# Swin block and plain attention block on one core: the plain block's order of work rewritten around two pairs of windows, with keys spread by transfers

## The reference

```python
def attention(xw, w_qkv, b_qkv, w_proj, b_proj):      # 8x8 windows, 6 heads of 16
    qkv = jnp.einsum('bhwc,cd->bhwd', xw, w_qkv) + b_qkv
    q, k, v = ...
    q = q * (1.0 / jnp.sqrt(jnp.float32(HEAD_DIM)))
    attn = jax.nn.softmax(jnp.einsum('bnhd,bmhd->bhnm', q, k), axis=-1)
    out = jnp.einsum('bhnm,bmhd->bnhd', attn, v).reshape(Bw, h, w, DIM_OUT)
    return jnp.einsum('bhwc,cd->bhwd', out, w_proj) + b_proj
# block:  x1 = x + attention(layernorm(x));  out = x1 + fc2(gelu(fc1(layernorm(x1))))
```

## Time and profile before

| | |
|---|---|
| median of three executions | 7636.98 us (7636.67 to 7640.51) |
| span of the profiled execution | 7641.6 us; no time of its own beside the span is listed |
| first block / second block | scores of the second block run from 4489.2 to 7598.5 us |
| PE busy over the span | 97% (7426.1 us) |
| DVE, ACT, POOL busy over the span | 83%, 84%, 67% |
| second block, 5500 to 6000 us: PE, DVE, ACT, POOL | 488, 398, 374, 282 us of 500 |
| granted TensorE clock there | 0.99 of full |
| 16 DMA engines there | 12% busy |

### The profile page before, as it was taken

One profiled execution on the slowest core, in us unless ns is written; L12 is line 12 of the kernel. 1 busy time (PEld: TensorE's weight loads), 2 busy tenths in 40 slices (PEclk: granted clock), 3 DMA queues, 4 the chain that ended last, 5 costly groups with the idle time before them and its releaser, 6 DMA issues. The chain is left out here.

```text
span 7641.6 us, 317406 instructions
## 1 busy us (share of the span) xinstructions
PE 7426.1 (97%) x113246; PEld 5558.8 (73%) x113246; DVE 6361.0 (83%) x13502; ACT 6423.1 (84%) x11836; POOL 5127.1 (67%) x6741
## 2 busy tenths in 40 slices
PE   7999999999999999999999969999999999999999
PEld 4777777777777777777777747777777777777776
DVE  5888888888888888888888848887887887887886
ACT  5999999999999999999999957777777777777777
POOL 3777777777777777777777745555555555555554
PEclk9999999999999999999999979999999999999999
DMA  0111111111111111111111001111111111111111
GB/s 21 29 29 31 30 30 29 30 30 29 30 29 30 30 29 30 29 30 30 29 30 30 27 20 27 27 27 27 27 27 27 27 27 27 27 27 27 27 27 25
DMA packets 342624, 214.43 MB, mean 28 GB/s; under 512 B 265624, under 2 KB 341144, under 8 KB 341144
## 3 DMA queue, kind: packets, MB, share of 16 engines
q1 hardware_dynamic: 341146, 194.49, 10.1%
HBM read 78.66 MB, written 77.07 MB: 20 GB/s over the span
## 5 line engine op out<-in xcount | busy, mean ns | idle before, releaser
L881 POOL TENSOR_TENSOR swin_score<-swin_score,swin_top 113x588 f32<-113x588 f32 x1024 | 1204.0, 1176 | 743.2 <-DVE swin_top L753 742.7
L624 ACT ACTIVATE swin_probT<-swin_ps_probs 128x339 f32<-128x339 f32 x2048 | 925.3, 452 | 197.3 <-PE swin_ps_probs L481 178.2
L1493 POOL TENSOR_TENSOR plain_k_heads<-plain_k_hat,plain_head_mask 96x128 f32<-96x128 f32 x1568 | 585.3, 404 | 647.7 <-ACT plain_k_hat L1357 647.7
L481 PE MATMUL swin_ps_probs<-swin_ident,swin_prob 113*128 113x113 f32 x6144 | 991.8, 270 | 6.7 <-ACT swin_probT L624 6.7
L481 PEld LDWEIGHTS swin_ps_probs<-swin_ident,swin_prob 113*128 113x128 f32 x6144 | 668.0, 141 | 355.2 <-issue 320.8
L748 DVE TENSOR_TENSOR swin_score<-swin_ps_scores,swin_bias_tab 113x588 f32<-113x588 f32 x1024 | 777.3, 759 | 175.7 <-PE swin_ps_scores L471 174.4
L753 DVE TENSOR_REDUCE swin_top<-swin_score 113x12 f32<-113x588 f32 x1024 | 768.8, 751 | 0.2
L630 ACT ACTIVATE swin_prob<-swin_score 113x588 f32<-113x588 f32 x1024 | 721.5, 705 | 5.8 <-POOL swin_score L881 2.9
L1334 ACT ACTIVATE plain_prob<-plain_score 128x384 f32<-128x384 f32 x784 | 409.6, 522 | 374.9 <-DVE plain_score L1402 372.7
L1318 ACT ACTIVATE plain_hid<-plain_ps_dense,plain_b_fc 128x512 f32<-128x512 f32 x588 | 405.3, 689 | 315.0 <-PE plain_ps_dense L1180 315.0
L784 DVE SCALAR_TENSOR_TENSOR swin_x<-swin_y,swin_y_rstd,swin_x_res 98x96 f32<-98x96 f32 x1024 | 602.1, 646 | 0.8 <-POOL swin_y_rstd L899 0.7
(11 more groups left out here) (187 smaller groups left out, 21172.4 us busy)
## 6 DMA issues: line engine op xcount, KB each, us to landing
swin_k_heads<-swin_k_hat SPq DMA_DIRECT2D x1024, 36.8 KB
plain_x_in<-between_blocks SPq DMA_DIRECT2D x784, 48.0 KB, 2.2
out_dram<-plain_x SPq DMA_DIRECT2D x784, 48.0 KB, 2.0
swin_x_in<-in_x SPq DMA_DIRECT2D x224, 136.5 KB
between_blocks<-swin_x SPq DMA_DIRECT2D x224, 136.5 KB
swin_x_in<-in_x SPq DMA_DIRECT2D x224, 19.5 KB
between_blocks<-swin_x SPq DMA_DIRECT2D x224, 19.5 KB
swin_x_in<-in_x SPq DMA_DIRECT2D x224, 2.6 KB
```

The costliest lines, as they stand in the source:

```text
L481: last = nc.tensor.transpose(psP[:, n * QT:(n + 1) * QT], prob[0:QT, p, 2 * hp:2 * hp + 2, :].rearrange('p h k -> p (h k)'), ident[0:QT, 0 ...
L624: nc.scalar.activation(to, psP[:, 0:3 * QT], ACT.Copy).then_inc(did['probT'], 1)
L881: nc.gpsimd.tensor_tensor(view, view, bcast(top[0:QT, p % 2, :], 2, WIN), ALU.subtract).then_inc(did['shifted'], 1)
L1493: last = nc.gpsimd.tensor_tensor(k_heads[0:DIM, (r + 1) % 2, w, :].rearrange('c (j k) -> c j k', j=J), bcast(k_hat[:, w * WIN:(w + 1) * WI ...
```

## The change

The first block and the launch stay. In the plain block:

- `score`, `top`, `prob` and `probT` get four buffers each, one for every pair of the group, in place of two.
- `scores(d, h)` makes the scores of two pairs at once (24 records), side by side in the three banks; `mix(d, h)` mixes two pairs at once and appends the sums. The four slots are gone; the body is one list of steps.
- The three chunks of the hidden layer stand behind one another; output is done for g-3, late in the body, not for g-4 early in it.
- `k_heads` is [128, 2, J, NT]: SP writes it with six transfers SBUF to SBUF in a group, 16 partitions of 2 KB each; everything else in it stays zero from set-up. `head_mask`, its load and POOL's eight products go.
- POOL does the normalisation of x1 (two operations of 384 elements) in place of DVE's four. The reciprocal on DVE is now that of pairs 0 and 1, Ln and Exp that of pairs 2 and 3.

```diff
-        k_heads = sb('k_heads', [128, 2, WINDOWS, J * WIN])
+        k_heads = sb('k_heads', [128, 2, J, NT])
-        score = sb('score', [128, 2, SC])
-        prob = sb('prob', [128, 2, heads, HALF])
-        probT = sb('probT', [128, 2, HP, QT])
+        score = sb('score', [128, PAIRS, SC])
+        prob = sb('prob', [128, PAIRS, heads, HALF])
+        probT = sb('probT', [128, PAIRS, HP, QT])
...
+                def spread(n, parity):
+                    sp.wait_ge(did['k_hat'], upto(n))
+                    sp.wait_ge(did['scored'], upto(n - 2, 1, 2))
+                    for band in range(BANDS):
+                        for j in range(J):
+                            rows = slice(32 * band + j * D, 32 * band + (j + 1) * D)
+                            sp.dma_start(k_heads[rows, parity, j, :], k_hat[rows, :]).then_inc(did['k_spread'], 16)
...
                 with sp.Fori(4, groups // 2) as m:
                     for k in range(2):
                         load(2 * m + k, k)
+                        spread(2 * m + k - 2, k)
                         store(2 * m + k - 8, k)
...
+                    def scores(d, h):
+                        if exists(g + d, groups):
+                            pe.wait_ge(did['q_hat'], upto(g + d))
+                            pe.wait_ge(did['k_spread'], spread_total(g + d))
+                            ug, uh = earlier_half(g + d, h)
+                            pe.wait_ge(did['shifted'], upto(ug, 2 * uh + 1, PAIRS))
+                            for p in (2 * h, 2 * h + 1):
+                                for half in range(2):
+                                    w = 2 * p + half
+                                    for band in range(BANDS):
+                                        part = slice(32 * band, 32 * band + 32)
+                                        last = nc.tensor.matmul(psS[half * HALF:half * HALF + WIN, band, p % 2 * BC:(p % 2 + 1) * BC], q_hat[part, parity(d), w * WIN:(w + 1) * WIN], k_heads[part, parity(d), :, w * WIN:(w + 1) * WIN], start=True, stop=True)
                             last.then_inc(did['scored'], 1)
...
+                    def mix(d, h):
+                        if exists(g + d, groups):
+                            pe.wait_ge(did['v_heads'], upto(g + d))
+                            pe.wait_ge(did['probT'], upto(g + d, 2 * h + 1, PAIRS))
+                            mg, mh = earlier_half(g + d, h)
+                            pe.wait_ge(did['mixedT'], upto(mg, mh, 2))
...
+                    scores(0, 0)
+                    mix(-1, 0)
+                    free(('v_heads', 0), ('hid', -4, 1, CHUNKS), ('x1', -3), ('k_hat', 0))
+                    keys(1, A)
+                    turn_probs(-1, 2)
+                    free(('x2', -4), ('hid', -4, 2, CHUNKS), ('q_hat', 0))
+                    queries(1, B)
+                    free(('k_hat', 1), ('v_heads', 0), ('hid', -4, 1, CHUNKS), ('x1', -3))
+                    project(-2, A)
+                    turn_probs(-1, 3)
+                    free(('q_hat', 1), ('x2', -4), ('hid', -4, 2, CHUNKS))
+                    hidden(-3, 0, B)
+                    free(('x1', -2), ('k_hat', 1), ('v_heads', 0), ('hid', -4, 1, CHUNKS))
+                    hidden(-3, 1, A)
+                    free(('hid', -3, 0, CHUNKS), ('q_hat', 1), ('x2', -4))
+                    hidden(-3, 2, B)
+                    scores(0, 1)
+                    mix(-1, 1)
+                    free(('hid', -3, 1, CHUNKS), ('x1', -2), ('k_hat', 1), ('v_heads', 0))
+                    values(1, A)
+                    turn_x(2)
+                    turn_probs(0, 0)
+                    free(('hid', -3, 2, CHUNKS), ('q_hat', 1), ('x2', -4))
+                    output(-3, B)
+                    turn_x1(-2)
+                    turn_probs(0, 1)
...
+                    copy_turned(-1, 1)
+                    high_x1(-3)
+                    exponentials(0, 0)
+                    bias_k(1, A)
+                    copy_turned(-1, 2)
+                    exponentials(0, 1)
                     act.preload_act_table_set(GELU_SET)
+                    copy_turned(-1, 3)
+                    gelu(-3, 0, B)
+                    gelu(-3, 1, A)
+                    gelu(-3, 2, B)
                     act.preload_act_table_set(EXP_SET)
+                    log_totals(-1, 1)
+                    exponentials(0, 2)
+                    invert_totals(-1, 1)
+                    spread_values(1, A)
+                    copy_x(2)
+                    high_x(2)
+                    copy_turned(0, 0)
+                    exponentials(0, 3)
...
+                    result(-4, B)
+                    shift(0, 0)
+                    low_x1(-3)
+                    shift(0, 1)
+                    bias_q(1, B)
+                    residual(-2, A)
+                    invert_totals(-1, 0)
+                    partial_x1(-2)
+                    normalise(-1, 0)
+                    moments_x1(-2)
+                    shift(0, 2)
+                    shift(0, 3)
+                    partial_x(3)
+                    normalise(-1, 1)
+                    moments_x(3)
+                    low_x(2)
...
+                    residual_x(1)
+                    power_x(2)
+                    norm_x(2)
+                    residual_x1(-2)
+                    power_x1(-2)
+                    norm_x1(-2)
```

More of the change, by code:

```diff
@@ L75 @@
     "sq_norm": "squared norms with their floor in SBUF", "log_norm": "their logarithm", "inv_norm": "1 / norm",
-    "reciprocal": "1 / sum of a group's last two pairs in the second block",
-    "k_heads": "a pair's keys spread over heads",
+    "reciprocal": "1 / sum of a group's first two pairs in the second block",
     "q_hat": "queries ready for the scores", "k_hat": "keys ready to be spread over heads",
@@ L1157, in _ @@
                     load(n, n % 2)
+                    if n >= 2:
+                        spread(n - 2, n % 2)
                 with sp.Fori(4, groups // 2) as m:
@@ L1184, in all_windows @@
                         return bass.AP(first.tensor, first.offset, [part, pair, [HALF, 2], column])
[L1186 to L1194, removed]
-                                    part = slice(32 * band, 32 * band + 32)
-                                    last = nc.tensor.matmul(psS[half * HALF:half * HALF + WIN, band, 0:BC], q_hat[part, r % 2, w * WIN:(w + 1) * WIN], k_heads[part, r % 2, w, :], start=True, stop=True)
-                            last.then_inc(did['scored'], 1)
@@ L1221, in turn_probs, with free @@
-                    def turn_probs(slot):
-                        tg, ts = before(g, slot, 1)
-                        if exists(tg, groups):
-                            pe.wait_ge(did['prob'], upto(tg, ts, PAIRS))
-                            rg, rs = before(tg, ts, 1)
-                            pe.wait_ge(did['probT'], upto(rg, rs, PAIRS))
+                    def free(*uses):
+                        for name, d, *place in uses:
+                            if exists(g + d, groups):
+                                pe.wait_ge(did[name], upto(g + d, *place))
+                                break
@@ new lines, in project, with hidden @@
+                    def project(d, bank):
+                        if exists(g + d, groups):
+                            pe.wait_ge(did['mixedT'], upto(g + d, 1, 2))
+                            for p in range(PAIRS):
+                                last = nc.tensor.matmul(psM[0:TT, bank, p * DIM:(p + 1) * DIM], mixedT[0:DIM, parity(d), p * TT:(p + 1) * TT], w_proj[0:DIM, :], start=True, stop=True)
+                            last.then_inc(did['proj_made'], 1)
+                    def hidden(d, c, bank):
+                        if exists(g + d, groups):
+                            pe.wait_ge(did['x1T_low'], upto(g + d))
+                            side = slice(c * 128, (c + 1) * 128)
+                            product(psM[:, bank, 0:NT], w_fc1_high[:, side], w_fc1_low[:, side], x1T_high[:, :], x1T_low[:, :]).then_inc(did['fc1_made'], 1)
@@ new lines, in output @@
+                    def output(d, bank):
+                        if exists(g + d, groups):
+                            pe.wait_ge(did['hid'], upto(g + d, CHUNKS - 1, CHUNKS))
+                            for p in range(PAIRS):
+                                for c in range(CHUNKS):
+                                    last = nc.tensor.matmul(psM[0:TT, bank, p * DIM:(p + 1) * DIM], hid[:, c, p * TT:(p + 1) * TT], w_fc2[:, c, :], start=c == 0, stop=c == CHUNKS - 1)
+                            last.then_inc(did['fc2_made'], 1)
@@ new lines, in spread_values @@
+                    def spread_values(d, bank):
+                        if exists(g + d, groups):
+                            act.wait_ge(did['v_made'], upto(g + d))
+                            act.wait_ge(did['mixed_made'], upto(g + d - 2, 1, 2))
+                            for odd in range(2):
```

(6 more changed lines are left out.)

515 lines of the change are left out of this document (228 added, 287 removed).

## The result

The changed kernel takes 7408.6 us (median of four, 7406.0 to 7413.4) against 7638.7 us before: a ratio of 0.970, 95% interval 0.968 to 0.971. That is 230 us less. The profiled execution took 7406.0 us, with a span of 7404.2.

A forecast was written before the change was run, and what follows sets the result against it. PE's own stream was taken as the bound: 15.75 us a group, −0.40 stalls, −0.92 shape changes, +0.5 wait on GELU 0, 14.95 us. Over 190 groups, with +5 once, this gave 7490 us, 8-in-10 range 7405 to 7600.

The forecast's parts named there:

- rival A: Hidden chunk 2 goes on at once without waiting for GELU 0: 7391 us at best, halfway 7440; chance 0.14.
- the wait on GELU 0: On PE, hidden chunk 2 must wait for ACT's first GELU to free a bank: +0.5 us in a group.
- PE's stream sets the pace: PE is busy 487.8 of 500 us in the second block, so savings must come from its own stream.
- Stalls that go, −0.40: PE's waits at the third slot's transposes (0.30 us) and the keys (0.10) vanish in each group, with a buffer per pair.
- Changes of shape, −0.92: Per group on PE, fewer products behind tiled work (−0.40), pair transposes behind mixes (−0.30), mixes before full-width work (−0.22).
- rival B: Shape changes on PE save nothing, only the stalls go: 7566 us, at worst 7661; chance 0.18.
- Scores have the same count and stay as they are: PE's scores, like projection, output, values and sums, cost the same after the change: no saving.
- The mix of the last pairs: PE's mix needs DVE's reciprocal: zero to 0.1 us late, taken as 0; decides only without the wait on GELU 0.
- Keys by transfers, zero: SP's six key transfers land at 10.1 us, wanted at 14.9 by the next scores: 4.8 us slack, zero cost.
- rival C: Key transfers served in series on SP's queue land late and delay PE's scores: 7815 us; chance 0.07.
- Rival D: ACT's unbroken row behind GELU 2 ends too late for the transposes of x1: 15.5 us a group, 7605 us; chance 0.08.
- Once, +5: The first group's keys come some 5 us later, a single cost at the second block's start.

The follow-up runs named there:

- e4: The changed kernel with the keys spread by POOL's eight products again in place of SP's transfers: 7392.3 us, ratio 0.968 to the kernel before.
- e12: The changed kernel with the key transfers behind the group's four stores on SP's queue: 7409.0 us, ratio 0.970 to the kernel before.
- e1: The kernel before with four score, top, prob and probT buffers and nothing else moved: 7644.9 us against 7641.5 us, ratio 1.0004.
- e3: The changed kernel with two score, prob and probT buffers in place of four: 8122 us, ratio 1.063 to the kernel before.
- e8: The changed kernel with the moves of e5 and e6, and the second scores split in two behind hidden chunks 0 and 1: 7479.8 us, ratio 0.980.
- e5: The changed kernel with ACT's exponentials of pair 1 behind the three GELUs and the second table load: 7382.0 us, ratio 0.966.
- e6: The changed kernel with pair 1's transposes ahead of those of x1 on PE at the body's end: 7366.4 us, ratio 0.964.
- e9: The changed kernel with the moves of e5 and e6, and pair 3's transposes between hidden chunks 1 and 2, their copy behind GELU 1: 7336.5 us.
- e2: The kernel before with the keys spread by six SP transfers in place of POOL's products, other engines' order untouched: 8544 us, ratio 1.118.
- e11: The changed kernel with ACT's two waits ahead of the biased keys in the other order: 7403.1 us, ratio 0.969 to the kernel before.

## Why the prediction was right, and where it was off

Forecast 7490 us in a range of 7405 to 7600; measured 7408.6, 3.6 us inside the fast edge of the range and near rival A's numbers, though not by its mechanism: the wait on GELU 0 is there. The main mechanisms are right, but the forecast had only 147 of the 230 us, and that the time still fell inside is in part luck, as the range reached down for a rival that did not come about. Point by point:

- *PE's stream sets the pace*: right. Each edit that took time out of PE's row showed in the result, and the engines with more or less work (POOL in e4, SP in e12) did not, but for the 16 us told of in e4.
- *Stalls that go, −0.40*: the size is borne out by the profile after, which has neither; the cause was wrong. I gave it to the four buffers. e1 shows that they give nothing alone, and e3 that ACT's new order can't run without them; it takes both.
- *Changes of shape, −0.92*: right, −0.96 by the rows after. They have 0.33 for every pair transpose, 0.24 and 0.23 for the first products of chunks 0 and 1 where no wait stands before them, 0.40 for the keys behind sums, 0.58 for 24 mix records. e8 puts two changes back and pays 0.57 without a wait. So rival B is out.
- *"Scores have the same count and stay as they are"*: this is the step that failed. 24 in one row take 0.61 us, not 2 x 0.39. Twice in a group that is 0.34 us, 67 us over 196 groups. The period as a whole was off by less, 14.95 against 14.71, because a wait that I missed (below) took 0.22 back. I took the saving of a second dozen in the same tiling for the mix, where a row showed it, and did not carry it to the scores. The same sentence left the projection and the output as they were; they cost 0.97 for 1.06 and 2.65 for 2.68 now that neither stands behind what it stood behind before, 0.12 together.
- *The wait on GELU 0, +0.5*: 0.57 from end to end, as the walk counted it. The walk came to the right moment through the wrong neighbour: I had DVE's two shifts as the last thing ahead, but ACT takes the exponentials of pair 1 behind the biased keys and a copy, and is free 0.3 us later than DVE is done. e5 shows the wait: 0.22 of the 0.45 between the starts goes when those exponentials leave the row.
- *A wait that I missed*: the first mix waits 0.22 us for ACT's copy of pair 1, whose transposes stand right ahead of the scores. e6 removes it.
- *The mix of the last pairs*: right that it decides only behind GELU 0 (e9).
- *Keys by transfers, zero, and rival C*: right but for the 0.09 us in a group that e4 shows. Six issues took 3.8 us and 2.0 to landing, side by side, not in series: the last landed 5.1 us behind the first issue. The fixed 2.0 us that the Trainium skill gives ("DMA: Bandwidth & Descriptors", the anatomy of one DMA) is there for a transfer issued by GpSimd; these are issued by SP and take the same 2.0. Its rule on transfers under 64 KB does not bear on the time here, because there are 5.8 us of slack. e2 is what it costs where there is none. (In rival C's sum, 0.9 x 190 + 5 is 176, not 180, and the range does not take in all of rival B, whose worst case is 7661; nothing hangs on either.)
- *Rival D, ACT late for the transposes of x1*: not seen; PE's waits after the change have no such row.
- *Once, +5*: not seen. The second block's first scores start at 4483.6 us, 5.6 earlier than before, but 4.4 of these lie in the first block, which is the same code and ended earlier in this execution; from its end to the first scores it is 48.5 us where it was 49.8.

Summed from end to end: 15.75 − 0.40 − 0.96 − 0.34 − 0.12 + 0.57 + 0.22 = 14.72 against a measured 14.71. The period's 1.04 us make 204 us over 196 groups, of the 237 between the two profiled spans (7641.6 and 7404.2). Most of the rest lies outside the steady pattern: 5.6 us ahead of the first scores; the second block's first three groups, 35.7 us for 48.1, at a granted clock of 0.91 for 0.69; and four turns of the unrolled loop, where two groups together last 32.0 to 34.7 us for 37.7 to 37.8 (29.4 and 31.5 without a turn).

## What to carry to other kernels

When a stream of matmuls is full, read what a piece costs behind each kind of neighbour, end to end, and price a reordering by that table, for every kind that is moved. Buffers and order are one design: four buffers alone changed nothing and the order alone lost 6%. A wait can cost more than the idle time shows (0.57 us for 0.30 before chunk 2), so take prices from end to end. Work moved to DMA is cheap only where its latency has slack, and a wait of 2.7 us on average on PE in every group cost the lowered clock on top of itself in most groups (e2).

## What the runs showed that was not expected

- A label in the chain or in the waits can name a bystander. The gap before chunk 2 was put down to the key transfers in 68 of 133 groups and as 5.8% of the chain over 30 us; with the transfers moved 3 us later (e12) or taken away (e4), the gap stayed and stood wholly with ACT.
- After 3 us of idle PE, and 1.4 us of work at full clock behind them, the granted clock was 0.61 over 4.4 us of full work (e2), where the kernel before has 0.99 over 500 us; the 24 output products took 4.47 us for 2.84. Over 5000 to 7000 us one group in about five kept the full clock.
- POOL's eight products made the kernel 12 to 16 us faster than SP's six transfers, on both versions in which the pair was run, with the landing of the transfers hidden. The time lies in the projection, which is held by ACT's later reading of the keys (0.97 us for 0.88). Why ACT is later is open; one suspected cause was tried (e11) and explains about 5 us at most.
